# A cross-attention layer in rounds of two steps, with four score banks and the next context in blocks of 1 MB

## The chip, the cores and the metric

The kernel runs on one core of one Trainium2 chip. The metric is the device time of one execution in microseconds (us). Data are float32; products marked fp32r are done as three products of parts (high by high, high by low, low by high), so that nearly full precision is kept.

## What is computed

Shapes: `x` is 4 x 128 x 512 (latents), `ctx` is 4 x 2048 x 512 (context). One layer of a Perceiver:

```
h  = x + cross_attention(layernorm(x), ctx)        # 16 heads of 64
h  = h + self_attention(layernorm(h))              # 16 heads of 32, head mask
out = h + mixture_of_attention_heads(layernorm(h)) # 16 experts, gated, causal
cross: q = LN(x) Wq + bq; k = ctx Wk + bk; v = ctx Wv + bv
       softmax(q k^T / 8) v, heads joined, times Wo, + bo
```

Most of the work is the cross attention: keys and values of 8192 context rows for 1024 columns each, in three fp32r products.

## The kernel before

**Data.** A batch's context, transposed, is held split into high and low parts in `ctxT` (2 x 4 x 2048 per partition). A *chunk* is 128 of its 2048 rows, 256 KB. Chunks and weight pieces arrive through four staging slots of 256 KB; ScalarE (ACT) writes the high part (L1299), VectorE (DVE, L1390) or GpSimd (POOL, L1087) writes raw minus high as the low part, and only then is the slot free for SyncE's next load (`part_free`).

**Steps.** The loop of the cross attention has 128 steps: 4 batches x 8 pairs of heads x 4 blocks of 512 context rows. Step t does on TensorE (PE):

- keys(t), L1183: 12 matmuls of 512 columns into one bank of a ring of four PSUM banks (0 to 3). ACT copies them with the bias to `kst` (L1361).
- scores(t-1), L1198: 8 small products (16 records of the trace) on 64 rows each, for two heads, into banks 4 and 5. ACT copies the scores to `prob` (L1371), DVE takes the running maximum (L1474). The next scores wait for both, since they overwrite the two banks.
- after a pair's four steps: turn_top (L1207) transposes the maxima, DVE reduces them (L1485), spread_top (L1213) spreads them over the partitions, DVE subtracts them from `prob` in two halves (L1492, "unit" = two steps' scores), ACT takes the exponential (L1377), DVE sums (L1501 to L1509).
- weigh, L1233: every second step the exponentials of a unit of four rounds (8 steps) earlier times V, with the sums by L1226; for the last two pairs the sums are done on PE by products with ones (L1235).
- four times in each half batch, four value chunks (L1161, 12 matmuls of 512 columns each, V for the next four pairs), copied by DVE (L1408); twice a batch the output product (L1171).

**Border.** Near the end of a batch the next batch's chunks overwrite `ctxT`, from four steps ahead on; behind the last batch come the self-attention weights in the same place, 4 of their 16 chunks multiplied by the head mask on POOL (L1096) before ACT may split them.

**Order.** Each engine runs its queue in program order, laid out by `Plan`: `products` (which value, output and tail products follow a step), `splits` (which chunk or weight is split in a step), `loads` (SyncE's order), and two tables written by hand: `TAIL_STEPS`, work of the self attention that is done inside the last steps, and `TAIL`, the order of what follows. Names there: sx transposes the normalized rows, pq/pk/sv project them for three batches, sl are logits, sr normalizes the softmax, sp transposes it, sw weighs, sf is the output projection, sh transposes, y and eo are the experts' products. The last normalization (ln3, sx3) needs the last output product (o).

## Time and profile before

| what | us |
|---|---|
| median of 3 runs (lowest, highest) | 1391.34 (1388.34, 1392.85) |
| the profiled execution | 1389.91 |
| its span in the trace | 1388.1 |
| PE busy | 1342.5 (97%) |
| DVE busy | 882.4 (64%) |
| ACT busy | 502.8 (36%) |
| POOL busy | 179.1 (13%) |
| first keys start, last keys' step starts | 81.43, 1073.63 |

The trace tells when each instruction of each engine began and how long it took. A merged row of the timeline ("start, duration, xcount") is a block of equal instructions; since matmuls overlap in the array, the cost of a block is the distance from its start to the start of the next block, not its duration. PEclk is the share of TensorE's full clock that was granted: 1.0 is 2.4 GHz, 0.5 is 1.2 GHz.

### The profile page before, as it was taken

The page shows a single profiled execution, that of the slowest core. Times are in us where ns is not written, and L with a number is a line of the kernel's source. Part 1 is how long each engine was busy: PE and PEld are TensorE (multiplying, and loading weights), DVE is VectorE, ACT ScalarE, POOL GpSimd, SP SyncE. Part 2 cuts the span into 40 slices and gives each one's busy share as a digit, 9 for nine tenths or more (in the row PEclk, how much of TensorE's full clock was granted, in tenths as well). Part 3 has the DMA queues.
Part 4 walks back from the last instruction along what each step waited for, and adds up shares of the span by engine and source line. Part 5 has one row for each costly group of instructions (what it writes and reads, how often), then busy time and mean ns, then how long its engine had stood idle before and what let it go on. Part 6 is the DMA issues. An engine that isn't in the chain of part 4 may idle for free.

```text
span 1388.1 us, 22386 instructions
## 1 busy us (share of the span) xinstructions
PE 1342.5 (97%) x9196; PEld 1095.4 (79%) x9196; DVE 882.4 (64%) x1280; ACT 502.8 (36%) x686; POOL 179.1 (13%) x140
## 2 busy tenths in 40 slices
PE   6999999999999999999999999999999987899999
PEld 5877888778878887887888777878887875688887
DVE  6426763695457448844763496457646457788779
ACT  4226541463135216521641264135313545312210
POOL 2211100140010004200100050011000500000030
PEclk9999999999999999999999999999999998799999
DMA  7401100240020004200100141010001321114300
GB/s 227 141 24 28 43 10 11 67 135 10 11 71 11 10 11 133 79 1 26 55 20 11 47 132 34 11 53 28 11 10 46 107 93 55 38 61 142 94 8 31
DMA packets 41107, 74.11 MB, mean 53 GB/s; under 512 B 6608, under 2 KB 10720, under 8 KB 39984
## 3 DMA queue, kind: packets, MB, share of 16 engines
q1 hardware_dynamic: 40096, 70.28, 16.4%
q0 software_dynamic: 912, 2.41, 0.6%
q8 instruction: 74, 1.21, 0.4%
q14 instruction: 25, 0.20, 0.0%
HBM read 69.53 MB, written 3.15 MB: 52 GB/s over the span
## 4 chain that ended last, share of the span: by engine, by line
PE 85%; DVE 9%; issue 2%; ACT 2%; DMA 1%; POOL 1%; SPq 0%; ACTq 0%; DVEq 0%
PE b_ps L1161 26%; PE b_ps L1183 21%; PE b_ps L474 9%; PE b_ps L1198 9%; PE b_ps L1233 7%; PE b_ps L500 3%; PE b_ps L397 3%; PE b_ps L1171 2%; PE b_ps L1259 2%; DVE b_mx L1474 1%; DVE b_prob L1492 1%; DVE b_sm L1501 1%; DVE b_ctxT L1390 1%; PE b_ps L1213 1%; DMA b_raw_v<-in_Wv 1%
## 5 line engine op out<-in xcount | busy, mean ns | idle before, releaser
L1183 PE MATMUL b_ps<-b_ctxT,wk 128*128 128x512 f32 x1536 | 385.8, 400 | 1.4 <-issue 1.4
L1161 PE MATMUL b_ps<-wv,b_ctxT 128*128 128x512 f32 x1536 | 361.2, 394 | 11.8 <-DVE b_ctxT L1390 11.7
L1161 PEld LDWEIGHTS b_ps<-wv,b_ctxT 128*128 128x128 f32 x1536 | 287.5, 189 | 75.8 <-issue 14.6
L1183 PEld LDWEIGHTS b_ps<-b_ctxT,wk 128*128 128x128 f32 x1536 | 280.9, 188 | 74.4 <-issue 12.0
L1361 ACT ACTIVATE b_kst<-b_ps,b_bkT 128x512 f32<-128x512 f32 x128 | 87.9, 687 | 452.0 <-PE b_ps L1183 451.0
L1408 DVE COPY b_V<-b_ps 128x512 f32<-128x512 f32 x128 | 88.3, 690 | 207.8 <-PE b_ps L1161 207.8
L1492 DVE TENSOR_TENSOR b_prob<-b_prob,b_ps 128x2048 f32<-128x2048 f32 x64 | 145.8, 2280 | 50.5 <-PE b_ps L1213 50.5
L1198 PE MATMUL b_ps<-b_q,b_kst 64*128 64x128 f32 x2048 | 148.7, 284 | 7.4 <-DVE b_mx L1474 7.4
L1198 PEld LDWEIGHTS b_ps<-b_q,b_kst 64*128 64x128 f32 x2048 | 124.5, 187 | 39.7 <-issue 36.0
L1371 ACT COPY b_prob<-b_ps 128x1024 f32<-128x1024 f32 x128 | 129.8, 1014 | 71.4 <-PE b_ps L1198 70.7
L1233 PE MATMUL b_ps<-b_prob,b_V 128*64 128x128 f32 x2048 | 138.6, 278 | 0.0
L1474 DVE TENSOR_TENSOR b_mx<-b_ps,b_mx 128x1024 f32<-128x1024 f32 x64 | 78.2, 1223 | 91.4 <-ACT b_prob L1371 91.4
L1377 ACT ACTIVATE b_prob<-b_prob 128x2048 f32<-128x2048 f32 x64 | 122.6, 1917 | 0.0
L1233 PEld LDWEIGHTS b_ps<-b_prob,b_V 128*64 128x64 f32 x2048 | 115.3, 138 | 8.6 <-issue 1.3
L1120 POOL TENSOR_TENSOR wk<-stage,wk 128x512 fp32r<-128x512 f32 x30 | 41.8, 1394 | 540.5 <-ACT wk L1307 540.5
L474 PE MATMUL b_ps<-b_ctxT,t_hhi 128*128 128x512 f32 x384 | 97.3, 391 | 0.0
L474 PEld LDWEIGHTS b_ps<-b_ctxT,t_hhi 128*128 128x128 f32 x384 | 71.5, 188 | 14.5
L1087 POOL TENSOR_TENSOR b_ctxT<-stage,b_ctxT 128x512 fp32r<-128x512 f32 x45 | 64.7, 1446 | 131.2 <-ACT b_ctxT L1299 131.1
L1501 DVE TENSOR_TENSOR b_sm<-b_prob,b_sm 128x1024 f32<-128x1024 f32 x60 | 75.0, 1251 | 3.1
L1120 POOL TENSOR_TENSOR wv<-stage,wv 128x512 fp32r<-128x512 f32 x28 | 39.2, 1401 | 216.4 <-ACT wv L1307 216.4
L595 ACT CAST b_ctxT<-t_raw 128x2048 fp32r<-128x2048 f32 x16 | 30.7, 1917 | 90.4 <-PE b_ps L474 72.2
L1299 ACT CAST b_ctxT<-stage 128x512 fp32r<-128x512 f32 x80 | 46.3, 620 | 25.3 <-DMA stage<-in_ctx 16.1
(206 smaller groups left out, 1203.1 us busy)
## 6 DMA issues: line engine op xcount, KB each, us to landing
stage<-in_ctx SPq DMA_DIRECT2D x64, 256.0 KB, 3.0
b_wo<-in_Wo SPq DMA_DIRECT2D x8, 1024.0 KB, 5.0
stage<-in_Wk SPq DMA_DIRECT2D x30, 256.0 KB, 2.7
stage<-in_Wv SPq DMA_DIRECT2D x28, 256.0 KB, 3.2
stage<-in_self_w SPq DMA_DIRECT2D x16, 256.0 KB, 2.8
t_raw<-in_q_proj SPq DMA_DIRECT2D x16, 256.0 KB, 4.5
t_raw<-in_k_proj SPq DMA_DIRECT2D x16, 256.0 KB, 3.2
t_raw<-in_v_proj SPq DMA_DIRECT2D x16, 256.0 KB, 3.5
```

What stands on the lines that cost most here:

```text
L474: mm = nc.tensor.matmul(ps, hh[:, b, c], ww[:, c], start=i == 0, stop=i == len(terms) - 1)
L1161: mm = nc.tensor.matmul(ps[:, G.bank[item]], ctxT[:, a, k, n * P:(n + 1) * P], wv[:, w, k], start=m == 0, stop=m == len(terms) - 1)
L1183: mm = nc.tensor.matmul(ps[:, G.bank["k", t]], wk[:, i % 2, w, k], ctxT[:, a, k, s * BANK:(s + 1) * BANK], start=m == 0, stop=m == len(ter ...
L1198: mm = nc.tensor.matmul(ps[:, SCB + h, c * P:(c + 1) * P], kst[rows, t % 2, c * P:(c + 1) * P], q[rows, i % 2], start=True, stop=True)
L1233: mm = nc.tensor.matmul(ps[rows, OB, 0:P], V[:, c, col:col + HD], weights, start=c == 0, stop=c == NC - 1)
L1361: nc.scalar.activation(kst[:, t % 2], ps[:, G.bank["k", t]], ACT.Identity, bias=bkT[:, i % NP:i % NP + 1]).then_inc(k_out, 1)
L1371: nc.scalar.copy(prob[:, unit % UNITS, :, s * SB:(s + 1) * SB], ps[:, SCB:SCB + 2].rearrange("p h (c t) -> p h c t", c=SB)).then_inc(s_out, 1)
L1377: nc.scalar.activation(p, p, ACT.Exp, scale=SCALE).then_inc(exp_done, 1)
L1408: nc.vector.tensor_copy(V[:, n], ps[:, G.bank[item]]).then_inc(v_out, 1)
L1474: nc.vector.tensor_tensor(mx[:], ps[:, SCB:SCB + 2].rearrange("p h (c t) -> p h c t", c=SB), so_far, ALU.max).then_inc(top_done, 1)
L1492: nc.vector.tensor_tensor(p, p, top, ALU.subtract).then_inc(sub_done, 1)
L1501: nc.vector.tensor_tensor(sm[:], blocks(2 * i + s // 2, s % 2), so_far, ALU.add).then_inc(sum_done, 1)
```

## The change

- **Rounds.** The loop goes over 68 rounds of two steps. A round does keys of both steps, then scores of both, then the weighing of the unit of four rounds earlier, then value chunks, output products and tail work. turn_top stands between keys and scores of every even round, spread_top between scores and weighing.
- **Banks.** Scores take banks 2 to 5, two for each step of a round, so scores(t) wait for what was done with scores(t-2). The ring for keys, values and output products is two banks (0 and 1) instead of four until the last step.
- **Values** come 6, 6 and 4 chunks in three rounds, instead of four times 4.
- **Context** is loaded by blocks of 1 MB (four chunks; the first block in four strided pieces of 256 KB with rows of 512 bytes) straight into the place of the low part; ACT splits from there and DVE/POOL write the low part over it. A block's load waits for the last keys and values that read that block. The staging slots hold weights alone.
- **Keys** take the order high-high, weight low, context low, and wait for the context's low part only ahead of the last four matmuls.
- **ACT and DVE** are laid out anew by round, the border's chunks by `CHUNK_STEPS`; DVE does all three sums of a pair in one odd round, both subtractions in one even round.
- **Tail.** The output product of the first four pairs moves to the border's round, and `TAIL_STEPS` and `TAIL` have another order: logits of the first batch, its softmax and two value projections stand inside the last rounds.

```diff
-    LAG_WEIGH, RING = 8, 4
+    LAG_WEIGH, RING, SCORE_BANKS = 4, 2, (2, 3, 4, 5)
...
-                self.products[half * h + 7 + n // SB].append(("v", h, n))
+                self.products[half * h + 4 + 2 * (n // 6)].append(("v", h, n))
...
-            groups = [(at + 27, 0, 4), (at + 42, 4, 8)]
+            groups = [(at + 31, 0, 4), (at + 42, 4, 8)]
...
+CHUNK_STEPS = (-3, -3, -3, -3, -2, -2, -1, -1, 0, 0, 0, 0, 1, 1, 1, 1)
...
+            def load_chunk(b, n):
+                if b > 0:
+                    sp.wait_ge(k_psum, STEPS * b - SB + n // SB + 1)
+                    sp.wait_ge(v_psum, NC * (2 * b - 1) + n + SB)
...
-                terms = [(a, w, k) for a, w in ((0, 0), (1, 0), (0, 1)) for k in range(C)]
+                terms = [(a, w, k) for a, w in ((0, 0), (0, 1), (1, 0)) for k in range(C)]
                 for m, (a, w, k) in enumerate(terms):
+                    if (a, k) == (1, 0) and t % STEPS < SB:
+                        chunk_lo(pe, b, SB * s + SB - 1)
...
-                if t > 0:
-                    pe.wait_ge(s_out, t)
-                    pe.wait_ge(top_done, (SB - 1) * ((t - 1) // SB) + (t - 1) % SB)
+                if t < 2:
+                    pe.wait_ge(v_out, NC)
+                else:
+                    pe.wait_ge(s_out, t - 1)
+                    pe.wait_ge(top_done, (SB - 1) * ((t - 2) // SB) + (t - 2) % SB)
...
+            for r in range(G.ROUNDS):
+                steps, unit = (2 * r, 2 * r + 1), r - G.LAG_WEIGH
+                complete = r // 2 - 1 if r % 2 == 0 else -1
+                if 2 * r < TOTAL:
+                    for t in steps:
+                        keys(t)
+                if 0 <= complete < NB * NP:
+                    turn_top(complete)
+                if 2 * r < TOTAL:
+                    for t in steps:
+                        scores(t)
+                if 2 * r < TOTAL and complete >= 0:
+                    spread_top(complete)
+                if unit >= 0:
+                    weigh(2 * unit)
+                    weigh(2 * unit + 1)
+                if 2 * r >= TOTAL and 0 <= complete < NB * NP:
+                    spread_top(complete)
+                for item in G.items(r):
...
+            for r in range(G.ROUNDS):
+                exponents = r % 2 == 1 and 0 <= r - 3 < 2 * NB * NP
+                key_first = any(item[0] == "ctx" for item in G.splits[2 * r])
+                if exponents:
+                    exponent(r - 3)
+                if 2 * r < TOTAL:
+                    key_out(2 * r)
+                for item in G.splits[2 * r]:
                     split_hi(item)
-                for item in G.products[t]:
+                if exponents and not key_first:
+                    exponent(r - 2)
+                if 2 * r < TOTAL:
+                    key_out(2 * r + 1)
+                if exponents and key_first:
+                    exponent(r - 2)
+                for item in G.splits[2 * r + 1]:
+                    split_hi(item)
+                if 2 * r < TOTAL:
+                    scores_out(2 * r)
+                    scores_out(2 * r + 1)
+                for item in G.late[r]:
+                    split_hi(item)
+                for item in G.items(r):
                     tail.scalar(act, X, item)
```

PE's queue in the steady part. Before, one pair of heads (four steps) without value chunks; L1183 is keys, L1207 turn_top, L1198 scores, L1213 spread_top, L1233 and L1226 weigh:

```order
L1183 MATMUL b_ps<-b_ctxT,wk 128x512 x12
L1207 MATMUL b_ps<-ident,b_mx 128x128 x2
L1198 MATMUL b_ps<-b_q,b_kst 128x128 x8
L1183 MATMUL b_ps<-b_ctxT,wk 128x512 x12
L1213 MATMUL b_ps<-ident,b_tops 128x128 x2
L1198 MATMUL b_ps<-b_q,b_kst 128x128 x8
L1233 MATMUL b_ps<-b_prob,b_V 64x128 x16
L1183 MATMUL b_ps<-b_ctxT,wk 128x512 x12
L1198 MATMUL b_ps<-b_q,b_kst 128x128 x8
```

The changed kernel, two rounds (four steps) of the same part; L1209 is keys, L1235 turn_top, L1226 scores, L1241 spread_top, L1261 and L1254 weigh:

```order
L1209 MATMUL b_ps<-b_ctxT,wk 128x512 x24
L1235 MATMUL b_ps<-ident,b_mx 128x128 x2
L1226 MATMUL b_ps<-b_q,b_kst 128x128 x16
L1241 MATMUL b_ps<-ident,b_tops 128x128 x2
L1261 MATMUL b_ps<-b_prob,b_V 64x128 x16
L1209 MATMUL b_ps<-b_ctxT,wk 128x512 x24
L1226 MATMUL b_ps<-b_q,b_kst 128x128 x16
L1261 MATMUL b_ps<-b_prob,b_V 64x128 x12
L1254 MATMUL b_ps<-b_total,b_ones 64x128 x2
L1261 MATMUL b_ps<-b_prob,b_V 64x128 x4
```

Keys and scores, which alternated, now stand in blocks of two steps: two blocks of each in four steps instead of four.

ACT's queue of the changed kernel in two rounds, odd then even; L1408 is the exponential, L1391 the copy of the keys, L1402 the copy of the scores, L1340 a weight's high part:

```order
L1408 ACTIVATE b_prob<-b_prob 128x2048 [waits b_sub_done]
L1391 ACTIVATE b_kst<-b_ps,b_bkT 128x512 [waits b_s_psum,b_k_psum]
L1408 ACTIVATE b_prob<-b_prob 128x2048 [waits b_sub_done]
L1391 ACTIVATE b_kst<-b_ps,b_bkT 128x512 [waits b_s_psum,b_k_psum]
L1402 COPY b_prob<-b_ps 128x2x512 [waits b_sum_done,b_pv_done,b_s_psum]
L1402 COPY b_prob<-b_ps 128x2x512 [waits b_s_psum]
L1391 ACTIVATE b_kst<-b_ps,b_bkT 128x512 [waits b_s_psum,b_k_psum] x2
L1402 COPY b_prob<-b_ps 128x2x512 [waits b_sum_done,b_pv_done,b_s_psum]
L1402 COPY b_prob<-b_ps 128x2x512 [waits b_s_psum]
L1340 CAST wk<-stage 128x512 [waits b_k_psum,b_filled1]
```

The second exponential now stands between the copies of the two steps' keys; before, an exponential stood behind the copy of the scores.

DVE's queue of the changed kernel in the first round with value chunks; L1524 to L1531 are the maxima, L1565 to L1574 the attention output, L1542 the subtractions, L1458 the copy of a value chunk:

```order
L1524 TENSOR_TENSOR b_mx<-b_ps,b_mx 128x1024 [waits b_top_done,b_s_out] x2
L1529 TENSOR_TENSOR b_mx<-b_mx 128x2x256 [waits b_top_done]
L1531 TENSOR_TENSOR b_mx<-b_mx 128x2x128 [waits b_max_half]
L1565 RECIPROCAL b_rb<-b_ps 128x128 [waits b_attn_done,b_pv_done]
L1567 TENSOR_TENSOR b_scaled<-b_ps,b_rb 128x128 [waits b_rb_done]
L1574 TENSOR_SCALAR b_attnT<-b_scaled,b_bvT 128x128 [waits b_o_free]
L1535 TENSOR_REDUCE b_tops<-b_ps 128x2 [waits b_turn_psum]
L1542 TENSOR_TENSOR b_prob<-b_prob,b_ps 128x2048 [waits b_spread_psum] x2
L1458 COPY b_V<-b_ps 128x512 [waits b_pv_done,b_v_psum] x6
```

Both subtractions now stand ahead of six copies, which free a ring of two banks.

## Rows read from the trace of the kernel before

**Rows 1.** The page, busy time of each engine and the clock in 40 slices.

```profile
PE 1342.5 (97%) x9196; PEld 1095.4 (79%) x9196; DVE 882.4 (64%) x1280; ACT 502.8 (36%) x686; POOL 179.1 (13%) x140
PEclk9999999999999999999999999999999998799999
```

**Rows 2.** Windows: loop, its end, self attention; length, busy per engine, PEclk, DMA.

```profile
81.43:1067.26 985.83, 977.03 (x7076) 792.01 (x7074) 598.84 (x659) 379.26 (x421) 123.69 (x87) 1.00 0.13 39
1067.26:1124.40 57.14, 55.24 (x531) 48.60 (x529) 27.89 (x32) 26.62 (x36) 22.17 (x22) 0.97 0.31 86
1124.40:1211.00 86.60, 67.46 (x508) 54.21 (x508) 69.89 (x199) 42.23 (x158) 0.00 (x0) 0.84 0.20 67
```

**Rows 3.** Timeline of PE, one pair without value chunks: start, duration, line.

```profile
422.10 1.53 PE L1233 MATMUL b_ps<-b_prob,b_V 128*64 128x128 f32 x24
...
424.21 3.06 PE L1183 MATMUL b_ps<-b_ctxT,wk 128*128 128x512 f32 x12
427.11 0.38 PE L1207 MATMUL b_ps<-ident,b_mx 128*128 128x128 f32 x2
427.42 1.16 PE L1198 MATMUL b_ps<-b_q,b_kst 64*128 64x128 f32 x16
428.51 3.04 PE L1183 MATMUL b_ps<-b_ctxT,wk 128*128 128x512 f32 x12
431.39 0.60 PE L1213 MATMUL b_ps<-ident,b_tops 128*128 128x128 f32 x4
431.92 1.16 PE L1198 MATMUL b_ps<-b_q,b_kst 64*128 64x128 f32 x16
433.01 1.97 PE L1233 MATMUL b_ps<-b_prob,b_V 128*64 128x128 f32 x32
434.91 3.04 PE L1183 MATMUL b_ps<-b_ctxT,wk 128*128 128x512 f32 x12
437.88 1.16 PE L1198 MATMUL b_ps<-b_q,b_kst 64*128 64x128 f32 x16
438.97 3.02 PE L1183 MATMUL b_ps<-b_ctxT,wk 128*128 128x512 f32 x12
441.92 1.16 PE L1198 MATMUL b_ps<-b_q,b_kst 64*128 64x128 f32 x16
```

**Rows 4.** Timeline of PE: the first two keys, with nothing between them.

```profile
81.43 5.60 PE L1183 MATMUL b_ps<-b_ctxT,wk 128*128 128x512 f32 x24
86.96 1.16 PE L1198 MATMUL b_ps<-b_q,b_kst 64*128 64x128 f32 x16
```

**Rows 5.** Timelines of ACT and DVE, the same pair.

```profile
440.02 1.92 ACT L1377 ACTIVATE b_prob<-b_prob 128x2048 f32<-128x2048 f32 x1
442.03 0.69 ACT L1361 ACTIVATE b_kst<-b_ps,b_bkT 128x512 f32<-128x512 f32 x1
...
432.03 2.29 DVE L1492 TENSOR_TENSOR b_prob<-b_prob,b_ps 128x2048 f32<-128x2048 f32 x1 [1.62 <-PE b_ps L1213]
```

**Rows 6.** Timeline of PE at a border: a wait for the maximum.

```profile
553.10 1.16 PE L1198 MATMUL b_ps<-b_q,b_kst 64*128 64x128 f32 x16 [1.42 <-DVE b_mx L1474]
```

**Rows 7.** Timeline of POOL, masked chunks of the self-attention weights.

```profile
1094.55 1.04 POOL L1096 TENSOR_TENSOR stage<-stage,t_hmT 128x512 f32<-128x512 f32 x1
...
1097.60 1.04 POOL L1096 TENSOR_TENSOR stage<-stage,t_hmT 128x512 f32<-128x512 f32 x1
```

**Rows 8.** Timeline of PE in the self attention: two of its waits.

```profile
1132.44 1.05 PE L402 MATMUL b_ps<-ident,t_prob 128*128 128x128 f32 x4 [3.93 <-DVE t_prob L715]
...
1207.92 4.43 PE L397 MATMUL b_ps<-b_ctxT,t_ao 128*128 128x512 f32 x12 [3.07 <-DVE t_ao L719]
```

**Rows 9.** DMA issues: KB each, median us from issue to landing, steady part.

```profile
stage<-in_ctx SPq DMA_DIRECT2D x32, 256.0 KB, 2.9
...
b_wo<-in_Wo SPq DMA_DIRECT2D x5, 1024.0 KB, 5.0
b_q<-q_s SPq DMA_DIRECT2D x22, 64.0 KB, 2.8
```

More of the change, by code:

```diff
@@ L116, in __init__ @@
         self.TOTAL = NB * self.STEPS
[L117 removed]
+        self.LAST = self.TOTAL + 7
+        self.ROUNDS = (self.LAST + 1) // 2
         self.HALVES = 2 * NB
@@ L143, in __init__ @@
         ring = [x for x in self.first if x[0] == "v"]
-        banks, last = deque(range(self.RING)), {}
+        banks, last = deque(range(4)), {}
         self.bank, self.earlier, self.nth, self.unit, counts = {}, {}, {}, {}, {}
@@ L169, in __init__ @@
                 place(x)
-        for t in range(self.LAST + 1):
-            if t == self.TOTAL:
-                for bank in (4, 5):
+        banks = deque(range(self.RING))
+        for r in range(self.ROUNDS):
+            if 2 * r == self.TOTAL:
+                for bank in self.SCORE_BANKS:
                     banks.append(bank)
                     last[bank] = ("s", self.TOTAL - 1)
-            for x in [("k", t)] * (t < self.TOTAL) + self.products[t]:
+            for x in [("k", t) for t in (2 * r, 2 * r + 1) if t < self.TOTAL] + self.items(r):
                 place(x)
@@ L1553, in _ @@
                     if item[0] == "ctx" and item[2] in LO_BY_DVE[item[1]]:
                         chunk_rest(item[1], item[2])
-                for item in G.products[t]:
+            for r in range(G.ROUNDS):
+                i = r // 2
+                if r % 2 == 0:
+                    if i - 1 in pairs:
+                        max_step(i - 1, 2)
+                        max_step(i - 1, 3)
+                        max_end(i - 1)
+                    if i - 3 in summed:
+                        attention_out(i - 3)
+                    chunks_rest(G.splits[2 * r])
+                    if i - 1 in pairs:
+                        max_rows(i - 1)
+                    chunks_rest(G.splits[2 * r + 1])
+                    if i - 1 in pairs:
+                        below_max(i - 1, 0)
+                        below_max(i - 1, 1)
+                else:
+                    if i in pairs:
+                        max_step(i, 1)
+                    chunks_rest(G.splits[2 * r])
+                    if i - 1 in summed:
+                        for s in range(1, SB):
+                            sum_step(i - 1, s)
+                        sum_end(i - 1)
+                    if i - 2 in pairs and i - 2 not in summed:
+                        attention_out(i - 2)
+                    chunks_rest(G.splits[2 * r + 1])
+                chunks_rest(G.late[r])
+                for item in G.items(r):
```

256 lines of the change are left out of this document (110 added, 146 removed).

## The prediction

> **What bounds the kernel now.** I read the page first: PE is busy 97% of the span and the clock is full but for four slices near the end [rows 1]. So time can be won only from what PE itself spends, from its few waits, and from the clock. Then the windows: the loop from the first keys to the last but one round takes 985.83 us, of which PE idles 8.8 (985.83 less 977.03) at full clock; the loop's end takes 57.1; the self attention behind it takes 86.6 with 19.1 idle and a mean clock of 0.84, which is part of the time at 1.2 instead of 2.4 GHz [rows 2]. Busy time hides the main thing, so I went to PE's timeline and took each block's cost as the distance to the next block's start [rows 3]. Keys cost 2.90 when turn_top follows, 2.88 ahead of spread_top, 2.97 and 2.95 ahead of scores. Two keys with nothing between them cost 5.53, and 24 matmuls at the spacing inside a block would cost little less [rows 4]: half of it, 2.77, is what keys cost without a change of form in front. So each time PE goes from the small float32 products to keys it loses 0.13 to 0.18, and going on to scores costs some 0.07 more. A scores block costs 1.09. Weighing costs 2.11 with the sums (422.10 to 424.21) and 1.90 without (433.01 to 434.91), turn_top 0.31, spread_top 0.53.
>
> One pair of heads, four steps, is therefore 2.90 + 0.31 + 1.09 + 2.88 + 0.53 + 1.09 + 1.90 + 2.97 + 1.09 + 2.95 + 1.09 + 2.11 = 20.91 us without value chunks [rows 3].
>
> **The change part by part.**
>
> *Rounds of two steps.* The numbers of products stay. The second keys of each round follow keys, and cost 2.72 to turn_top (5.62 less 2.90; a block of 12 products in one form costs that wherever it repeats, since 5.53 is 2.72 twice and 0.09 for the step on to scores) or 2.79 to scores. Keys of four steps: 2.90 + 2.72 + 2.97 + 2.72 = 11.31, where they were 11.70. Gain 0.39. (In the odd round the step on to scores is in the 2.97.)
>
> *Two scores in a row.* The weighing shows what small products cost inside a block: 24 records in 1.36 (422.10 to 423.46), so 0.057 a record, and 16 of scores would take 0.91. The rest of 1.09, 0.18, belongs to coming and going, and two in a row pay it once. Bounds: 4.36 for the four scores of a pair if nothing merges, 4.00 if all does. I take 4.00, because the second scores' one new wait, for the copy of the second keys, ends in time: that copy starts 0.11 after the first scores (442.03 against 441.92) and takes 0.69 [rows 3, 5], so it is over 0.80 in, and the second scores start 0.91 in. It is close: 0.1 of slack in odd rounds, 0.4 in even ones, where turn_top stands ahead.
>
> The Trainium skill (TensorEngine Tiling (Array Packing), Key Properties) says that changing the tiling mode drains the engine. By it a pair pays for its changes of mode, 10 before and 7 now (spread_top between scores and weighing keeps two); at 0.18 each that is 0.54 a pair, 17 us in all and 1364 in the end, where the rows give a time for each neighbour separately; the trace before has no spread_top between those two, so it can't decide.
>
> A pair: 20.91 - 0.39 - 0.36 = 20.16, gain 0.75. From the first keys to the last round there are 31.5 pairs: **-23.6 us**. With nothing merged in the scores it would be -12.3.
>
> *Value chunks.* Three entries a half batch instead of four, but keys behind values paid no entry, and three such keys instead of four are left. It cancels to 0.1 us. The ring of two banks asks DVE to copy chunk n before chunk n+2. A chunk is 2.72 of PE, so the third starts 5.4 after the first; DVE must have copied the first by then. In the even rounds DVE has both subtractions in front (2.25 each), the first starting about 0.64 after spread_top (432.03 against 431.39) [rows 3, 5], so it is free 5.1 after spread_top; the third chunk wants its bank 0.53 + 1.90 + 5.44 = 7.9 after. Slack 2: cost nothing; the cover is PE's weighing and two chunks.
>
> *ACT.* In odd rounds without values in front, the first exponential starts 3.0 after spread_top and ends at 4.9; the copy of the first keys runs 5.5 to 6.2; the second exponential (1.92 [rows 5]) to 8.1; the copy of the second keys is due at 8.25. Slack 0.1 again. Where a value weight is split between them (once in a half batch, 0.62) the copy is 0.5 late and the second scores wait 0.35: 7 x 0.35 = **+2.5**.
>
> *Waits in the loop.* The 8.8 us idle are mostly at the first steps and at the borders, where scores waited for the maximum because DVE and ACT had the chunks' splits in front (1.42 at one border) [rows 2, 6]. With two sets of score banks that wait has two steps of slack. What is late next: the first keys of the new batch. Their block's load can start only after the old batch's keys 2 rounds earlier (12 us of slack behind the other keys, scores and weighing); 1 MB lands in 5.0 [rows 9], the four splits take 2.5 and the last low part 1.4 more, ending about 10 after those keys, inside that round and the next. The three later blocks have more. I count **-8.8 + 1.8**: the 1.8 are new, in the last batch, where the ring's bank of the output product is freed by DVE only after ln2, which waits for sx1 behind that product.
>
> *SP's and POOL's queues.* SP's block loads wait for keys, and what is queued behind them (weights four steps ahead, q two rounds ahead) keeps a round or more of slack. POOL does eight or fewer chunks at a border as before.
>
> *Start.* The first two chunks are on the path to the first values. They come in rows of 512 bytes: four times as many pieces. Rows bound it [rows 9]: 64 KB in such rows took 2.8, no more than 256 KB in rows of 2 KB (2.9), so the gain or loss per piece may be 0; if time went by pieces, 512 of them would be like the 1 MB transfer, 5.0 instead of 2.9, +2.1. I take **+0.5**, nearer to the equal rows. The Trainium skill (DMA: Bandwidth & Descriptors, Specifications) puts line rate at 512 B and above; by it this term would be 0.
>
> *The end.* I followed each engine from the last pair's first keys. New waits of PE: 2.7 for sx2's parts ahead of pq0 (ACT has the scores' copies in front), 2.0 ahead of the logits, because ACT stands in the masked chunks' chain (3.05 for each of four chunks, 1094.55 to 1097.60 [rows 7]) and the copies of pk3 come after two exponentials, and 3.0 ahead of sx3, which needs the last output product and ln3. Against them stand the 1.9 before and the 3.93 that the transposes waited [rows 8]. sx3 comes 4 us earlier than before, and the logits' softmax and both value projections lie behind it already, 7 us of DVE work that stood in a stretch where DVE is busy 69.9 of 86.6 [rows 2]. Bounds: 0, if all of that is given back in waits for DVE; 18, if half of the 19.1 idle and most of the loss at 1.2 GHz go. I take **-7** (the 4 and as much again of the 7 as DVE's share of the waits allows, 3).
>
> Sum: -23.6 + 2.5 - 7.0 + 0.5 - 7.0 = -34.6 from the profiled 1389.9, so 1355.3. The median of the runs lies 1.4 above the profiled execution: **1357 us**.
>
> **The rivals.**
>
> *A, the scores do not merge.* The slack of 0.1 in each round is not there: the release and the load of weights behind it take longer, and the two scores cost 2.18 again; DVE gives nothing back in the end. -12.3 + 2.5 - 7.0 + 0.5 + 0 = -16.3: 1375. For it: the closeness. Against it: a released scores block after a maximum started at once.
>
> *B, the end gives more.* All the loss at 1.2 GHz goes with PE's waits: -18 instead of -7, 1346. For it: the low clock came only where PE had waited [rows 2, 8]. Against: three waits of 2 to 3 us are new.
>
> *C, value copies become the bound.* If DVE reaches the copies two subtractions (4.5) later than I have it, in each of the 14 even rounds with values, PE waits 4.5 less the slack of 2: 14 x 2.5 = 35 given back, 1392, no change. For it: DVE is the busiest engine beside PE [rows 1]. Against: its work in such a round is no more than in others.
>
> *D, slower: ACT's second exponential.* The copy of the second keys is queued behind the second exponential, which waits for DVE's second subtraction. If that comes late in the odd rounds, the second scores wait for up to a whole exponential: 31.5 x 1.92 = 60, giving 1357 + 60 = 1417. It outweighs the gain from 1.1 us in each odd round on. For it: by my schedule there is only 0.1 of slack, and half the rounds have no values to give cover. Against it: subtractions start at a fixed 0.64 behind spread_top.
>
> *E, the change acts on nothing:* scores hardly wait for the copies and maxima in the steady part [rows 3], so the banks by themselves free nothing, and if blocks in a row cost what they cost apart, only the borders' 7.0 remain: 1389.9 - 7.0 + 3.0 = 1386, plus 1.4. Against it stands the 5.53 of the two keys [rows 4]; I give it no chance of its own.
>
> **How the numbers follow.** Chances: the forecast 0.55, A 0.20, B 0.12, C 0.06, D 0.07. A difference under 0.3%, 4 us, is about what a measurement cannot tell from none. Faster: forecast, A, B and a little of C: 0.88; same: 0.05; slower: 0.07. Range: from B, 1346, to A, 1375, which leaves C and D out.
>
> **What would show it.** Keys in blocks of 24 records at 5.6 and scores in blocks of 32 at 2.0, a pair at 20.2: right. A scores block of 32 at 2.2, or a wait of PE for ACT's `kst` copy: A or D, by its size. PE waiting for DVE's `b_V` copy: C. The clock behind the loop (0.84 before) tells B. The prediction is wrong if a pair takes over 20.6, or if PE waits at a border for chunks.

## The result and the profile after

| what | before | after |
|---|---|---|
| median, us (lowest, highest) | 1390.00 (1388.34, 1392.85), 4 runs | 1372.26 (1371.43, 1374.70), 4 runs |
| the profiled execution, us | 1389.91 | 1371.43 |
| its span, us | 1388.1 | 1369.6 |

The ratio is 0.9873, 95% interval 0.9851 to 0.9896: the change gains 1.3%. Forecast were 1357 in a range of 1346 to 1375, a gain of 34 us; 18 came. For the profiled execution, which took 1371.4, the forecast's sum was 1355.3: 16.1 us are missing.

The page of the changed kernel, the busy times and the clock [rows 1]:

```profile
PE 1320.4 (96%) x9196; PEld 1091.7 (80%) x9196; DVE 891.1 (65%) x1280; ACT 496.4 (36%) x686; POOL 174.9 (13%) x140
PEclk9999999999999999999999999999999999899999
```

PE does the same instructions in 22 us less. That is more than the kernel gained, so part of it went into waiting.

PE's timeline of the changed kernel, one pair of heads without value chunks [rows 3]:

```profile
415.06 5.78 PE L1209 MATMUL b_ps<-b_ctxT,wk 128*128 128x512 f32 x24
420.68 0.38 PE L1235 MATMUL b_ps<-ident,b_mx 128*128 128x128 f32 x2
420.99 2.06 PE L1226 MATMUL b_ps<-b_q,b_kst 64*128 64x128 f32 x32
422.97 0.71 PE L1241 MATMUL b_ps<-ident,b_tops 128*128 128x128 f32 x4
423.61 1.97 PE L1261 MATMUL b_ps<-b_prob,b_V 128*64 128x128 f32 x32
425.51 5.74 PE L1209 MATMUL b_ps<-b_ctxT,wk 128*128 128x512 f32 x24
431.18 2.06 PE L1226 MATMUL b_ps<-b_q,b_kst 64*128 64x128 f32 x32
433.16 1.53 PE L1261 MATMUL b_ps<-b_prob,b_V 128*64 128x128 f32 x24
...
435.28 1.21 PE L1209 MATMUL b_ps<-b_ctxT,wk 128*128 128x512 f32 x4
```

From start to start: keys 5.62 and 5.67 (forecast 5.62 and 5.69), scores twice 1.98 (forecast 2.00), turning 0.31, spreading 0.64 (forecast 0.53), weighing 1.90 and 2.12. The pair takes 20.22 us, before 20.91, forecast 20.16. Both merges came as they were worked out.

The windows of the loop, its end and the self attention [rows 2], with the same borders in the program (length; busy time of PE, PEld, DVE, ACT, POOL; PEclk; DMA share; GB/s):

```profile
80.29:1061.73 981.44, 965.17 (x7128) 796.00 (x7126) 613.16 (x665) 377.12 (x426) 119.33 (x88) 1.00 0.12 39
1061.73:1116.00 54.27, 51.49 (x515) 46.01 (x514) 28.86 (x39) 28.27 (x63) 22.27 (x22) 1.00 0.27 92
1116.00:1195.00 79.00, 63.98 (x482) 51.26 (x481) 63.31 (x184) 37.50 (x126) 0.00 (x0) 0.87 0.18 58
```

The loop, first keys to the keys of step 126, is only 4.4 us shorter (981.44 against 985.83), and its idle time grew from 8.8 to 16.3 us. (By its end the changed order has done one more unit of weighing and one more scores block, 3.1 us of work, so like for like it is 7.5 shorter.) The forecast's terms for the loop add up to a fall of 28.1 (23.6 less 2.5, and 7.0). What follows, keys of step 126 to the end, fell from 320.8 (1388.1 less 1067.26) to 307.9 us, 9.9 like for like where 7 was forecast; the first keys start 1.1 earlier (80.29 against 81.43), where 0.5 later was forecast; one execution can't resolve that, since the eleven kernels of the experiments, which start alike, had them at 80.38 to 82.89.

To find the loop's loss I took the waits of PE between the first step and 1030 us, in both kernels. First before, then after (us in total, times, longest):

```profile
PE b_ps L1198 <- DVE b_mx L1474: 5.5, 7, 1.4
PE b_ps L1207 <- DVE b_mx L1481: 1.9, 2, 1.3
PE b_ps L1183 <- issue: 1.4, 1, 1.4
```

```profile
PE b_ps L1241 <- DVE b_tops L1535: 7.6, 3, 2.5
PE b_ps L1235 <- DVE b_mx L1531: 3.8, 9, 0.7
PE b_ps L1226 <- ACT b_kst L1391: 1.5, 2, 0.7
PE b_ps L1226 <- DVE b_mx L1524: 0.8, 3, 0.3
```

There are now three waits of 2.5 us, one per border, for the reduction of the turned maxima (`b_tops`). Here is the second border, timeline of all engines:

```profile
549.34 2.51 POOL L1112 TENSOR_TENSOR b_ctxT<-b_ctx_raw,b_ctxT 128x512 fp32r<-128x512 f32 x2 [7.97 <-ACT b_ctxT L1331]
...
549.83 0.88 DVE L1574 TENSOR_SCALAR b_attnT<-b_scaled,b_bvT 128x128 f32<-128x128 f32 x1
549.86 2.06 PE L1226 MATMUL b_ps<-b_q,b_kst 64*128 64x128 f32 x32
...
550.63 3.45 DVE L1441 TENSOR_TENSOR b_ctxT<-b_ctx_raw,b_ctxT 128x512 fp32r<-128x512 f32 x2
552.06 3.14 POOL L1112 TENSOR_TENSOR b_ctxT<-b_ctx_raw,b_ctxT 128x512 fp32r<-128x512 f32 x2 [0.20 <-ACT b_ctxT L1331]
...
554.00 0.41 DVE L1535 TENSOR_REDUCE b_tops<-b_ps 128x2 f32<-128x256 f32 x1
...
554.33 3.09 DVE L1441 TENSOR_TENSOR b_ctxT<-b_ctx_raw,b_ctxT 128x512 fp32r<-128x512 f32 x2
554.46 1.04 PE L1241 MATMUL b_ps<-ident,b_tops 128*128 128x128 f32 x4 [2.55 <-DVE b_tops L1535]
...
555.43 3.25 PE L1261 MATMUL b_ps<-b_prob,b_V 128*64 128x128 f32 x32
```

PE had turned the maxima at 549.9, but DVE's queue holds the low parts of chunks 8 and 9 ahead of the reduction, and these take 1.7 us each, not 0.69. At the second and third border the clock then falls to 1.2 GHz for 3.4 us, so the weighing takes 3.18 where it takes 1.90. The view of DVE's instructions by tile, before and after, shows what changed (min/median/max ns):

```profile
L1390 DVE TENSOR_TENSOR b_ctxT<-stage,b_ctxT x35: 673/687/1783, 10.9 to 1081.2; 128x512 fp32r<-128x512 f32 x35
```

```profile
L1441 DVE TENSOR_TENSOR b_ctxT<-b_ctx_raw,b_ctxT x35: 674/1417/1780, 10.3 to 1066.7; 128x512 fp32r<-128x512 f32 x35
```

I call a stall what a block of PE costs above the least that such a block costs elsewhere with the same neighbours. The loop's stalls are 8.2 us before and 20.0 after. The 20.0 are: borders 13.7 (three reductions 7.8, the low clock behind them 3.2, scores late before and behind the borders 2.6), the maxima late in the round behind an output product 2.5 (three times), the maxima late elsewhere 2.4, the first steps 1.4.

The waits for the maxima have a part in common with the borders. In seven of those rounds (behind the three output products, and at 133, 258, 519 and 781 us) the last maximum, which reads and writes SBUF alone, stands beside a low part of a value weight on POOL:

```profile
398.34 1.72 POOL L1144 TENSOR_TENSOR wv<-stage,wv 128x512 fp32r<-128x512 f32 x1 [6.86 <-ACT wv L1340]
398.95 1.39 DVE L1531 TENSOR_TENSOR b_mx<-b_mx 128x256 f32<-128x256 f32 x1
```

It takes 1.39 to 1.49 us there, and 0.42 where POOL is idle: 1.0 us more, and PE's stall is 0.82 in three of these rounds and 0.38 in four.

Two causes were to be tested: what DVE has in its queue at a border, and why its low parts are slow.

### The profile page after: what moved, and what is told of

Its sections match the earlier page's. It is cut to its first block, busy times and chain, and to the rows that moved or that the text cites. A ratio compares the mean times of both kernels' runs of the same rounds, so it can differ in the third digit from the quotient of the medians.

```text
span 1369.6 us, 22355 instructions
## 1 busy us (share of the span) xinstructions
PE 1320.4 (96%) x9196; PEld 1091.7 (80%) x9196; DVE 891.1 (65%) x1280; ACT 496.4 (36%) x686; POOL 174.9 (13%) x140
## 4 chain that ended last, share of the span: by engine, by line
PE 86%; DVE 11%; issue 2%; DMA 1%; ACT 0%; SPq 0%; DVEq 0%
PE b_ps L1185 26%; PE b_ps L1209 19%; PE b_ps L483 9%; PE b_ps L1226 9%; PE b_ps L1261 9%; PE b_ps L406 3%; PE b_ps L509 3%; DVE b_mx L1524 3%; PE b_ps L1195 2%; PE b_ps L1287 2%; PE b_ps L1241 1%; DVE b_prob L1542 1%; DVE b_ctxT L1441 1%; DVE b_mx L1531 1%; DVE b_mx L1529 1%
## 5 line engine op out<-in xcount | busy, mean ns | idle before, releaser
L1185 PE MATMUL b_ps<-wv,b_ctxT 128*128 128x512 f32 x1536 | 358.4, 393 | 11.1 <-DVE b_ctxT L1441 11.1
L1209 PE MATMUL b_ps<-b_ctxT,wk 128*128 128x512 f32 x1536 | 366.9, 394 | 1.2 <-DVE x L1466 1.2
L1209 PEld LDWEIGHTS b_ps<-b_ctxT,wk 128*128 128x128 f32 x1536 | 285.8, 188 | 68.4 <-issue 8.3
L1391 ACT ACTIVATE b_kst<-b_ps,b_bkT 128x512 f32<-128x512 f32 x128 | 87.9, 687 | 508.2 <-PE b_ps L1209 508.0
L1458 DVE COPY b_V<-b_ps 128x512 f32<-128x512 f32 x128 | 88.3, 691 | 218.1 <-PE b_ps L1185 218.1
L1542 DVE TENSOR_TENSOR b_prob<-b_prob,b_ps 128x2048 f32<-128x2048 f32 x64 | 143.5, 2283 | 57.6 <-PE b_ps L1241 57.6
L1261 PE MATMUL b_ps<-b_prob,b_V 128*64 128x128 f32 x2048 | 139.7, 279 | 0.2 <-issue 0.2
L1408 ACT ACTIVATE b_prob<-b_prob 128x2048 f32<-128x2048 f32 x64 | 122.4, 1914 | 42.7 <-DVE b_prob L1542 42.7
L1402 ACT COPY b_prob<-b_ps 128x1024 f32<-128x1024 f32 x128 | 124.2, 1015 | 35.7 <-PE b_ps L1226 35.6
L1226 PEld LDWEIGHTS b_ps<-b_q,b_kst 64*128 64x128 f32 x2048 | 120.3, 187 | 20.3 <-issue 18.1
L1226 PE MATMUL b_ps<-b_q,b_kst 64*128 64x128 f32 x2048 | 133.8, 279 | 2.3 <-ACT b_kst L1391 1.5
L1261 PEld LDWEIGHTS b_ps<-b_prob,b_V 128*64 128x64 f32 x2048 | 116.4, 139 | 8.1 <-issue 0.9
L1524 DVE TENSOR_TENSOR b_mx<-b_ps,b_mx 128x1024 f32<-128x1024 f32 x64 | 78.1, 1220 | 8.8 <-ACT b_prob L1402 5.5
L1112 POOL TENSOR_TENSOR b_ctxT<-b_ctx_raw,b_ctxT 128x512 fp32r<-128x512 f32 x45 | 62.1, 1393 | 109.5 <-ACT b_ctxT L1331 109.4
L604 ACT CAST b_ctxT<-t_raw 128x2048 fp32r<-128x2048 f32 x16 | 30.7, 1917 | 86.8 <-PE b_ps L483 69.9
L483 PE MATMUL b_ps<-b_ctxT,t_hlo 128*128 128x512 f32 x192 | 51.4, 389 | 0.0
```

The source lines that it names most:

```text
L483: mm = nc.tensor.matmul(ps, hh[:, b, c], ww[:, c], start=i == 0, stop=i == len(terms) - 1)
L1185: mm = nc.tensor.matmul(ps[:, G.bank[item]], ctxT[:, a, k, n * P:(n + 1) * P], wv[:, w, k], start=m == 0, stop=m == len(terms) - 1)
L1209: mm = nc.tensor.matmul(ps[:, G.bank["k", t]], wk[:, i % 2, w, k], ctxT[:, a, k, s * BANK:(s + 1) * BANK], start=m == 0, stop=m == len(ter ...
L1226: mm = nc.tensor.matmul(ps[:, SCB + 2 * (t % 2) + h, c * P:(c + 1) * P], kst[rows, t % 2, c * P:(c + 1) * P], q[rows, i % 2], start=True, ...
L1261: mm = nc.tensor.matmul(ps[rows, OB, 0:P], V[:, c, col:col + HD], weights, start=c == 0, stop=c == NC - 1)
L1391: nc.scalar.activation(kst[:, t % 2], ps[:, G.bank["k", t]], ACT.Identity, bias=bkT[:, t // SB % NP:t // SB % NP + 1]).then_inc(k_out, 1)
```

## The experiments

Each stands on the changed kernel unless it says otherwise; differences are between medians, and ratios are to the kernel before. The names in brackets are those by which the expectations speak of each other's kernels.

**1. The reduction first (e1_rows_first).** In DVE's even rounds:

```diff
+                    if i - 1 in pairs:
+                        max_rows(i - 1)
                     chunks_rest(G.splits[2 * r])
-                    if i - 1 in pairs:
-                        max_rows(i - 1)
                     chunks_rest(G.splits[2 * r + 1])
```

> In each of the three border rounds the reduction of the turned maxima (b_tops) goes ahead of the low parts of chunks 8 and 9 in DVE's queue. Theory Q (the 2.6 us wait of PE ahead of the spread is DVE's queue order): the three waits fall from 2.62 us to under 0.3, the weigh blocks behind them lose the 1.6 us that they had extra at the lower clock in two of the borders, so 3 x 2.4 + 2 x 1.6 = 10 us less than the changed kernel: about 1362. Rival T (DVE's time in that round decides, whatever its order): the low parts of chunks 8 and 9, now 0.4 us later, or the subtractions, unchanged at 557.3 us, hold PE one round later instead, and the total moves by under 2 us: 1371. In both, DVE's low parts beside POOL's stay at 1.6 to 1.7 us each.

Measured: 1377.84 us (ratio to the kernel before 0.9909, 0.9895 to 0.9924), 5.6 **slower** than the change. The waits for `b_tops` are gone; what follows at the second border on DVE and then on PE:

```profile
555.09 6.52 DVE L1441 TENSOR_TENSOR b_ctxT<-b_ctx_raw,b_ctxT 128x512 fp32r<-128x512 f32 x4
...
561.53 4.47 DVE L1542 TENSOR_TENSOR b_prob<-b_prob,b_ps 128x2048 f32<-128x2048 f32 x2
```

```profile
566.38 2.01 PE L1226 MATMUL b_ps<-b_q,b_kst 64*128 64x128 f32 x16 [2.13 <-ACT b_kst L1391]
```

PE no longer waits there: the next keys start 4.8 us after the turning (553.68 to 558.51) where it was 9.1 (2.6 of wait and 1.6 of low clock less). But the subtractions still start late; ACT's exponential waits for them, and the copy of the keys (`kst`) is queued behind that exponential. The scores then wait 2.1 us. Theory Q is refuted as a cure. T has the mechanism right, DVE's time in that round decides, and its size too small. PE's waits up to 1030 us sum to 14.4 us, against 13.7 in the changed kernel, so they alone would cost next to nothing. What is new is the clock: it stood at 1.2 GHz for 17.1 us of the loop instead of 6.8, and 10.2 us more at half the rate are 5.1 of the 5.6. This is the mechanism of rival D, at the borders only.

**2 and 3. Who makes the low parts (e2_low_dve, e3_low_pool).** `LO_BY_DVE` for the borders, with `lo_counts` adjusted to count any split (the comments number the two edits):

```diff
-    LO_BY_DVE = [set(range(0, NC, 2))] + [{0, 2, 4, 6, 8, 9, 12, 13}] * (NB - 1) + [{0, 2, 4}]
+    LO_BY_DVE = [set(range(0, NC, 2))] + [{0, 2, 4, 6, *range(8, 16)}] * (NB - 1) + [{0, 2, 4}]   # 2: all by DVE
+    LO_BY_DVE = [set(range(0, NC, 2))] + [{0, 2, 4, 6}] * (NB - 1) + [{0, 2, 4}]                  # 3: none of 8..15
```

> All low parts of chunks 8 to 15 of a border go to DVE (8 in place of 4), POOL makes none of them; order unchanged, so four of them (not two) stand ahead of the reduction. Theory B (DVE and POOL slow each other when both make low parts from SBUF: 0.68 us alone, 1.65 us together): each of DVE's takes 0.68 to 0.75 us, the four ahead of the reduction take 2.8 us where two took 3.45, and PE's wait falls from 2.62 to about 2.0 us; total about 1370. Rival R (a low part read from the raw block costs DVE 1.7 us by itself, or waits for ACT's splits): four take 6.6 us, PE's wait rises to about 5.8 us, the total by 3 x 3.2 + what the clock takes, to about 1384.

> The other side: all low parts of chunks 8 to 15 of a border go to POOL, none to DVE. Nothing stands ahead of the reduction, so PE's 2.62 us wait is gone at each border. Theory B (each slows the other): POOL's low parts take 1.1 us each while DVE makes no two-input operation in SBUF, and 1.6 to 1.8 us while it does; eight take 9 to 12 us from 549.3, so the last lands between 558 and 561.5. Keys of the next round need chunk 11 at about 558 and chunk 15 at about 561: no wait at 1.1 us each, up to 2 us a border at 1.7. Total 1362 to 1368. Rival: POOL's low parts take 1.7 us or more whatever DVE does: the last at 563, waits of 2 to 4 us a border, 1368 to 1375.

Measured: all by DVE 1366.98 (0.9827, 0.9811 to 0.9844); all by POOL **1360.62** (0.9785, 0.9768 to 0.9803). The second border of the two, DVE in the first and POOL in the second:

```profile
549.44 2.49 DVE L1442 TENSOR_TENSOR b_ctxT<-b_ctx_raw,b_ctxT 128x512 fp32r<-128x512 f32 x4
...
551.85 0.42 DVE L1536 TENSOR_REDUCE b_tops<-b_ps 128x2 f32<-128x256 f32 x1
...
552.32 0.71 PE L1242 MATMUL b_ps<-ident,b_tops 128*128 128x128 f32 x4 [1.00 <-DVE b_tops L1536]
```

```profile
546.29 10.16 POOL L1113 TENSOR_TENSOR b_ctxT<-b_ctx_raw,b_ctxT 128x512 fp32r<-128x512 f32 x8 [6.94 <-ACT b_ctxT L1332]
...
548.98 0.41 DVE L1536 TENSOR_REDUCE b_tops<-b_ps 128x2 f32<-128x256 f32 x1
```

With POOL out of the way DVE makes *four* low parts ahead of the reduction in 2.49 us, where *two* beside POOL took 3.45, and PE's wait falls from 2.6 to 1.0 us. Rival R is refuted: ACT splits at the same time in both, so it isn't ACT, nor the new place of the raw block. With all on POOL nothing stands ahead of the reduction, the wait is gone, and the clock stays up. POOL's low parts take 1.27 us each (10.16 for eight), the last ends at 556.5, in time. Both totals are better than theory B had them: the first by 3.0 us (PE's wait is 1.0, not 2.0, and the clock stays up), the second by 1.4. Theory B holds in both, and the two engines together are slower than DVE alone: four and four took from 549.3 to 557.4 (8.1 us), eight on DVE alone from 549.4 to 554.7 (5.2 us).

**4. The last sum later (e4_sum_later).** `sum_end` of a pair moves from the odd round to the next even round, behind `max_end`.

> The last sum (b_total) moves from the odd round to the even round behind it, after the maxima, so that DVE's queue no longer stands before the maxima until PE has weighed the pair before. Theory: the waits of PE for the turned maxima at 133, 258, 519 and 781 us (0.37 each) and those behind the output product at 394, 656 and 917 (0.82 each) go, as does part of the 1.02 at 301: 4 to 5 us less, 1367.5. Rival: the maxima are late because the scores and DVE's own sums are, not because of that wait; total within 1 us of the changed kernel.

Measured: 1372.90 (0.9876, 0.9859 to 0.9894), no change. The profiled execution was its slowest, 1375.25. Two of its waits of PE up to 1030 us:

```profile
PE b_ps L1241 <- DVE b_tops L1535: 10.0, 6, 2.9
PE b_ps L1235 <- DVE b_mx L1531: 1.9, 3, 0.6
```

Six of the nine waits for the maxima are gone, as expected, so `b_total` ahead of the maxima, which waits for PE's weighing, was a condition of theirs. The three behind the output products stay, against expectation: there DVE has the addition to the residual and the statistics ahead of the maxima (1.3 us), and the last maximum still takes 1.39 beside POOL. No run moved POOL's weight low parts, so whether that alone would end these waits is not shown. And the sum, put ahead of the reduction, lengthens the three waits for `b_tops` by 0.3 us each and opens three new ones. Right cause, wrong new place.

**5. Keys apart (e5_keys_apart).** On kernel 3 (e3_low_pool), the two weigh blocks of a round go between its two keys.

```diff
                 if 2 * r < TOTAL:
-                    for t in steps:
-                        keys(t)
+                    keys(2 * r)
+                if unit >= 0:
+                    weigh(2 * unit)
+                    weigh(2 * unit + 1)
+                if 2 * r < TOTAL:
+                    keys(2 * r + 1)
```

> Stands on e3_low_pool, whose loop is nearly free of waits (1360.6 us). The two weigh blocks of a round move between its two blocks of keys, so that no two blocks of keys follow each other; scores stay merged, nothing is added or taken away. Theory M (blocks of the same kind in a row cost less: 0.39 us a pair of heads for the keys, by which the forecast was made): 31.5 x 0.4 = 12 us more, 1373. Rival (a block costs the same wherever it stands, and the shorter pair comes from the waits that the rounds removed): 1361, with two blocks of keys and what follows them unchanged at 2 x 2.8 us.

Measured: 1495.97 (1.0745, 1.0726 to 1.0764), 135 us more; neither theory. DVE and PE in the even rounds:

```profile
433.95 0.29 DVE L1569 TENSOR_TENSOR b_scaled<-b_ps,b_rb 128x128 f32<-128x128 f32 x1
...
434.34 0.33 PE L1262 MATMUL b_ps<-b_prob,b_V 128*64 128x128 f32 x2 [4.59 <-issue]
```

The first weighing of a pair overwrites the bank which `b_scaled` of the pair before still reads, and DVE comes to that only behind the maxima: 86.5 us of such waits in 25 places. In the changed kernel the scores stand between. The granted clock averaged 0.963, where kernel 3 has 0.991: it stood at 1.2 GHz for 75 us of the loop and in kernel 3 for none, which costs another 37.5. The run spoils its own comparison; only its undisturbed blocks can be read: keys 2.91, 2.86, 2.99 and 2.95, spreading 0.47, together 12.17 a pair, where kernel 3 has 5.62, 5.66 and 0.64, 11.92.

**6. Keys apart in odd rounds only (e12_keys_odd),** where no bank is waited for.

> Stands on e3_low_pool. As e5_keys_apart, but in odd rounds only, where weigh does not wait for the bank that DVE frees late in an even round (that wait, 3 to 5 us, is what spoiled e5). Nothing added, nothing taken away. Theory M (two blocks of keys in a row cost less than two apart): by e5's undisturbed blocks 0.2 to 0.3 us a pair of heads, 6 to 9 us in all, 1367 to 1370. Rival (blocks cost the same wherever they stand): within 1.5 us of 1360.6.

Measured: 1373.71 (0.9885, 0.9871 to 0.9898), 13.1 more than kernel 3. In the steady part two pairs take 73.64 us instead of 73.25 (keys of step 48 to those of 56, with one set of value chunks), so 0.195 a pair. Other pairs give 0.12 to 0.23, and all of them outside the borders together about 5 us: just under M's lower bound. Another 6 us are at the borders, 2.1 each: PE has done the weighing already when it comes to the new element's keys, and then waits 1.56 us for the maxima, whose last one again takes 1.38 beside POOL. 1.8 us lie behind the last keys. The rival is refuted by the blocks; the total is above what I expected since I hadn't counted the borders.

**7. The end's tables (e6_tail_before, e9_tail_order).** The tables of the kernel before, then only its order behind the rounds.

```diff
-TAIL_STEPS = {115: "lr0 lr1 lr2", 117: "lr3 lr4", 120: "ln0", 121: "ln1 gate xl0 sx0", 122: "ln2", 123: "xl1 sx1",
...
+TAIL_STEPS = {114: "lr0", 116: "lr1 lr2", 122: "lr3 lr4 ln0", 123: "gate sx0 xl0", 124: "ln1", 125: "xl1 ln2 sx1",
...
```

> The changed kernel with the two tables of the kernel before for the end (order and steps of the tail's operations; its last entry, sv0, at step 135, since the rounds end there). Theory W (the tables were what made the end shorter, by the four waits that the forecast named): from the keys of step 126 to the end 9 to 13 us more, total 1382 to 1385. Rival G (the rounds themselves shorten the end, by the two steps less and the four score banks that come free; the tables give little): under 4 us more, 1372 to 1376.

> The changed kernel with its own table of steps, but what follows the last round in the order of the kernel before (the operations that already stand in the steps left out). It parts the 20 us that e6_tail_before cost. Theory O (order behind the rounds): from the last keys to the end e6 needed 320.0 us and the changed kernel 302.5; without the two waits that e6 opened inside the steps, 7.5 and 4.4 us, this run keeps the waits 3.9, 2.7, 2.1 and 3.1 us and the low clock behind them: 5 to 9 us more than the changed kernel, 1377 to 1381. Rival S (all of it is the steps): within 2 us of the changed kernel, 1371 to 1374.

Measured: both tables 1392.36 (1.0008, 0.9997 to 1.0019), **20.1 more** than the change; the order alone 1383.25 (0.9950, 0.9937 to 0.9964), 11.0 more. Windows from the last keys' last matmul to the end, of the change, the old order, both old tables:

```profile
1067.08:1369.60 302.52, 280.73 (x1744) 233.91 (x1742) 230.67 (x555) 89.07 (x211) 33.32 (x23) 0.97 0.21 70
```

```profile
1068.44:1382.10 313.66, 287.34 (x1744) 239.41 (x1742) 231.49 (x555) 89.59 (x211) 33.31 (x23) 0.95 0.20 68
```

```profile
1070.31:1390.30 319.99, 286.90 (x1744) 238.04 (x1742) 231.09 (x554) 89.87 (x211) 33.42 (x23) 0.95 0.20 66
```

The old order costs 11.1 us in this stretch: 4.5 more idle (26.3 against 21.8) and 6.6 more busy with the same 1744 matmuls, which is the clock (0.95 against 0.97). The waits are those of before again, among them PE's 3.07 for `t_ao` [rows 8]. The remaining 9 us of the first run are the steps' table, with two new waits of 11.9 us together, of which 3.8 are won back in the rounds just before:

```profile
1063.00 1.04 PE L411 MATMUL b_ps<-ident,t_xn 128*128 128x128 f32 x4 [4.43 <-DVE t_xn L667]
1082.88 0.69 PE L1235 MATMUL b_ps<-ident,b_mx 128*128 128x128 f32 x2 [7.49 <-DVE b_mx L1531]
```

Of the first run's theories W named the right place and was too small, G is refuted; of the second's, O holds and was 2 us too small, S is refuted: the tables are worth more than the whole gain at the end. The rounds with the old tables give back all that they win in the loop, since normalizations and maxima then meet in DVE's queue.

**8. The product out of the border (e7_product_even).** On kernel 3, `groups = [(at + 32, 0, 4), (at + 40, 4, 8)]` in place of 31 and 42.

> Stands on e3_low_pool. The output products of the first three elements move from steps 31 and 42 (odd rounds) to 32 and 40 (even rounds), so that DVE's addition to the residual (0.69 us) and its statistics no longer stand ahead of the last two maxima of a pair. Theory: the 0.8 us that PE waits for the turned maxima behind the product at 392, 649 and 907 us go, and nothing takes their place: 2.4 us less, 1358.2. Rival: the product's place is what hides the border (PE has 1.2 to 3.7 us more of work ahead of it), so that moving it behind the border's keys opens a wait at the border for the first chunks of the new element, 1 to 3 us each: 1361 to 1367.

Measured: 1375.39 (0.9871, 0.9853 to 0.9889), 14.8 more than kernel 3. PE at the second border:

```profile
551.28 0.44 PE L1236 MATMUL b_ps<-ident,b_mx 128*128 128x128 f32 x2 [3.13 <-DVE b_mx L1532]
551.65 3.69 PE L1227 MATMUL b_ps<-b_q,b_kst 64*128 64x128 f32 x32
```

The rival's cover is real, larger than expected (4.8 us a border), and it is not the chunks that are late but the maxima: DVE's round before the border fits only if PE has the product's 3.1 us to do. Part of it is again POOL, which now starts the next low parts while the maxima still run: their last two steps take 1.18 and 1.37 us, in kernel 3 0.69 and 0.42. The clock fell again (scores 3.69 instead of 2.06), at all three borders. The 0.8 us behind the second products did go.

**9. All sixteen low parts to POOL (e8_pool_all),** on kernel 3, `[set()] * (NB - 1)`.

> As e3_low_pool, and the low parts of chunks 0, 2, 4 and 6 of the three borders go to POOL too: all sixteen. Theory B (DVE and POOL slow each other, 0.65 us becomes 1.7 on DVE): DVE's maximum of the odd round ahead of the border is no longer late, the 0.53 us of PE before its second scores go (three times), total 1359. Rival: POOL becomes the bound, 16 low parts at 1.3 us = 21 us from about 530 us to 551, chunk 7 later than the 548 at which the second keys of the element want it: waits of up to 2 us a border, 1361 to 1367.

Measured: 1367.50 (0.9820, 0.9804 to 0.9837), 6.9 more than kernel 3. The time is the rival's, but not its path. POOL at the second border:

```profile
538.99 7.40 POOL L1113 TENSOR_TENSOR b_ctxT<-b_ctx_raw,b_ctxT 128x512 fp32r<-128x512 f32 x4
```

POOL makes these four in 7.40 us, 1.85 each, since DVE's sums run beside them; still the last of them, chunk 7's, is done at 546.4, in time. What is late is DVE, whose sums are slowed as much:

```profile
539.57 4.00 DVE L1552 TENSOR_TENSOR b_sm<-b_prob,b_sm 128x1024 f32<-128x1024 f32 x2 [2.92 <-ACT b_prob L1409]
...
545.27 1.40 DVE L1560 TENSOR_TENSOR b_total<-b_sm 128x256 f32<-128x256 f32 x1
...
552.14 0.44 PE L1236 MATMUL b_ps<-ident,b_mx 128*128 128x128 f32 x2 [1.79 <-DVE b_mx L1532]
```

In kernel 3 the two take 3.44 and 0.42, and the sum between them (1.64 here) 0.69. So PE waits 1.79 us for the maxima: from the new element's first keys to the turning are 7.96 us, in kernel 3 5.90, and the scores behind take 0.4 more. The 0.53 ahead of each border did go.

**10. The three findings together (e11_product_40):** kernel 3 with chunks 0 and 2 to POOL as well (`[{4, 6}]`), `sum_end` behind both subtractions, second product at step 40, first left at 31.

> Stands on e3_low_pool and tries to beat it, with three edits: the low parts of chunks 0 and 2 of a border to POOL as well (4 and 6 stay on DVE, since e8_pool_all made chunk 7 late), the last sum b_total behind both subtractions of the even round, and the second output product of an element at step 40 in place of 42 (the first stays at 31, in the border, where e7_product_even showed it is needed). Theory: the 0.53 us ahead of each border, the 0.35 us at 135, 260, 517 and 775, the 0.90 at 949 and the 0.8 us behind each second product go: 6 us less than e3_low_pool's 1360.6, 1354 to 1355.5. Rival: POOL with two more chunks, or attnT of the last pair at step 40, is late: the chunk costs up to 1.7 us a border, the product 1 to 2 us each: 1359 to 1365.

Measured: **1356.23 us** (0.9759, 0.9746 to 0.9772), 16.0 less than the change, faster than both kernels. The three largest of PE's waits up to 1030 us:

```profile
PE b_ps L411 <- DVE t_xn L667: 1.3, 1, 1.3
PE b_ps L1242 <- DVE b_tops L1536: 1.1, 3, 0.4
PE b_ps L1236 <- DVE b_mx L1532: 1.0, 3, 0.3
```

Chunk 7 had been in time in experiment 9 after all; taking load off POOL was right for DVE's sake. 4.4 us came of the 6 expected, 0.7 short of the theory's range and outside the rival's. Of the difference, 1.1 are the new waits of 0.4 us for `b_tops`, one at each border.

## Why the prediction was right, and where it was not

- **Rounds and scores merge: right, both.** A pair gained 0.69 where 0.75 was forecast, 21.7 us over the loop instead of 23.6. Spreading cost 0.64 instead of 0.53, because weighing now follows it instead of scores; the rows before had no such neighbours. Rival A, which I gave 0.20, is refuted: PE waits for `kst` 1.5 us in all. The keys' part of it was measured apart (experiment 6): 0.195 a pair for one of the two merges, and 0.39 was forecast for both. The scores' part shows in the blocks alone (1.98 for two, 1.09 for one); no run parted them again.
- **The rule on modes:** the Trainium skill (TensorEngine Tiling (Array Packing), Key Properties) led to 0.54 a pair; the trace has 0.69, between that and my 0.75. It can't be parted into modes and neighbours here: experiment 6 has one change of mode a pair more, which at 0.18 gives nearly its 0.195 too.
- **ACT's copies, +2.5: right in place, too large.** In seven rounds, the seven that were named, a value weight's split and the exponential stand ahead of the second keys' copy, and the two scores take 2.11 instead of 1.98 (515.14 to 517.25): 0.13 each, 0.9 in all, where 0.35 each was forecast. Rivals C and E fell with the trace (no wait for `b_V`; the pair is shorter), D in the steady part, though experiment 1 shows its mechanism once DVE is late.
- **Waits in the loop, -7.0: this step failed.** The 8.8 of before became 22.6: 20.0 in the blocks and 2.6 for normalized rows and the residual (1.33 and 1.24, at 1036 and 1051 us), where I had 1.8 in all. (That is more than the 16.3 idle, since the low clock and a wait inside a block of records don't show as idle.) So +13.8 where -7.0 was forecast. I looked for what would be late next and named the first keys of the new batch, their load and their low parts; nothing of that was late, though 1 MB of context took 6.7 us to land (median of 15) and not the 5.0 of the sum. The error was in a sentence that isn't there: I never priced DVE's queue ahead of the reduction in the border round. "The last low part 1.4 more" was near enough for one chunk, but two of DVE's low parts stand ahead of `max_rows`, and beside POOL's they take 1.7 each. The trace of before held both numbers (maximum 1783 against a median of 687 in the tile view); I took no row for it. Experiments 3 and 10 close the account: without the waits of the border, and in the second without most others, the kernel stands at 1360.6 and 1356.2, and 1357.0 was forecast.
- **Output product in the border:** not priced at all. It is worth 4.8 us a border on kernel 3.
- **The end, -7: mis-sized,** it was 9.9. And its source was unseen: the rounds with the old tables would have made the end worse, the new tables are worth 20 us. Clock and waits moved together, as rival B had it, but only in part (PEclk 0.84 before, 0.87 after in the self attention). In all, the end has 20.5 us at 1.2 GHz where it had 30.7, and at half the rate those 10.2 us are 5.1 of the 9.9.
- **Start, +0.5: not settled.** It came out at -1.1 in the profiled execution, but the start moves by up to 2.6 us between executions of kernels that start alike (80.29 to 82.89). Neither a cost nor a gain of the rows of 512 bytes can be read from that, and they weren't tried apart.

Together: 20.8 us too little from waits in the loop, 1.9 from the pairs, less 1.6 (ACT's copies), 2.9 (the end) and 1.6 (the start, which may be scatter) that turned out better: 16.6, where 16.1 are missing.

Of the two signs of being wrong, a pair over 20.6 didn't come (20.22). PE did not wait at a border *for* chunks, which was the second, but for the reduction behind two chunks in DVE's queue, and a sign for that was not set. That the result lies in the range is in part luck: its upper end, 1375, was worked out for scores that don't merge, and they did. What used up half of the gain stood under no rival.

## What to carry to other kernels

Where a change frees PE, follow each other engine's queue through the busiest round instruction by instruction, with durations taken where its neighbours are the ones it will have: a queue's order decides only if its sum fits. Work for DVE and POOL that reads only SBUF is better given to one of them at a time than shared, and then placed where the other has no such work either (experiment 9). A hand-made order for an end belongs to the loop that leads up to it: when the loop changes, lay it anew, and price the old order on the new loop before crediting either.

## What the runs showed of the hardware

**DVE and POOL hold each other up, by operand.** In the changed kernel a DVE low part (two inputs from SBUF) takes 683 ns on average in the 12 instances without POOL and 1612 in the 12 wholly beside a POOL operation (1415 to 1780). The addition to `attnT`, SBUF only, takes 0.29 alone and 0.85 to 0.88 at the three borders beside POOL (1.24 in kernel 3); the last maximum, SBUF only, takes 0.42 alone and 1.39 to 1.49 beside POOL. Operations that read one operand from PSUM don't change: without POOL and wholly beside it, the maximum takes 1219 and 1211 ns (92 and 3 instances), the subtraction 2274 and 2283 (6 and 4). POOL's own low part takes 1.28 us alone or beside those, up to 1.78 beside DVE's. By the Trainium skill (SBUF — State Buffer, SBUF: two separate sides) GpSimd and a DVE operation with two SBUF inputs share one pair of ports, which the first to start holds for its whole instruction. The trace agrees in kind: full turns would make each take 0.68 + 1.28 = 1.96 us where both queues are full, and each takes up to 1.78.

**A wait can be paid for again in the clock.** A border's 2.6 us of waiting was followed by 3.4 us at 1.2 GHz at two of three borders, 1.6 us more each; at the first border the same wait left the clock up. Experiment 1 had almost the same sum of waits and 10.2 us more at 1.2 GHz, so the sum of waits alone doesn't price a change.
